# Seven products of summed sub-blocks in place of eight plain ones, in the second layer of a two-layer graph network on one Trainium2 core

## What is computed

```
x = layernorm(x + relu((adj / rowsum) @ x @ Wn.T + bn + x @ Ws.T + bs))
x = layernorm(x + relu(d * (adj @ (d * x)) @ W1 + b1))     d = rowsum ** -0.5
```

## Time and profile before

| what | value |
|---|---|
| median of 3 runs | 784.59 us (783.98 to 784.97) |
| the profiled execution, its own time | 784.35 us |
| its span, first to last instruction | 782.7 us |
| time outside the span | 1.65 us |
| TensorE matmul busy | 774.9 us (99%), 3672 instructions |
| VectorE busy | 597.9 us (76%), 951 instructions |
| ScalarE busy | 388.2 us (50%), 537 instructions |
| DMA | 160.93 MB, mean 206 GB/s |

### The profile page before, as it was taken

How to read it: one execution, slowest core, us unless ns; L and a number is a source line. 1 busy time by engine, 2 the same in 40 slices (tenths; PEclk the granted TensorE clock), 3 DMA queues, 4 the chain that set the end, 5 groups by cost and what they waited for, 6 DMA issues and landing times.

```text
span 782.7 us, 11147 instructions
## 1 busy us (share of the span) xinstructions
PE 774.9 (99%) x3672; PEld 647.7 (83%) x3672; DVE 597.9 (76%) x951; ACT 388.2 (50%) x537; POOL 2.5 (0%) x14
## 2 busy tenths in 40 slices
PE   9999999999999999999999999999999999999996
PEld 5888888888888888888888888888888888888886
DVE  6999999999899998998967565565646556564554
ACT  5644645646355464454644545454444545544452
POOL 0000000000000000000000000000000000000000
PEclk9999999999999999999999999999999999999999
DMA  7965574756646566475575656657574666657541
GB/s 297 340 242 190 197 260 162 246 183 198 231 151 244 171 200 237 149 244 186 187 246 176 231 171 215 213 189 242 171 248 150 211 213 194 236 180 242 165 165 52
DMA packets 54059, 160.93 MB, mean 206 GB/s; under 512 B 5008, under 2 KB 17936, under 8 KB 54032
## 3 DMA queue, kind: packets, MB, share of 16 engines
q1 hardware_dynamic: 45536, 151.41, 57.2%
q10 hardware_dynamic: 8352, 9.05, 3.4%
q0 software_dynamic: 144, 0.13, 0.1%
HBM read 152.17 MB, written 8.39 MB: 205 GB/s over the span
## 4 chain that ended last, share of the span: by engine, by line
PE 99%; DVE 0%; ACT 0%; issue 0%
PE ps_main L875 87%; PE ps_epi L795 6%; PE ps_epi L783 2%; PE ps_main L897 1%; PE ps_main L854 1%; PE ps_epi L786 1%; PE ps_main L842 1%; PE ps_epi L907 0%; DVE tt L531 0%; PE ps_epi L816 0%; DVE tt L552 0%; ACT ps_epi L418 0%; ACT tt L432 0%; DVE xs L773 0%; PE ps_epi L916 0%
## 5 line engine op out<-in xcount | busy, mean ns | idle before, releaser
L300 ACT ACTIVATE hi<-raw 128x1024 fp32r<-128x1024 f32 x254 | 268.9, 1059 | 277.2 <-PE ps_main L875 243.5
L474 DVE TENSOR_TENSOR lo<-raw,hi 128x1024 fp32r<-128x1024 f32 x254 | 310.3, 1222 | 98.0 <-ACT hi L300 97.8
L875 PE MATMUL ps_main<-hi,xs 128*128 128x512 f32 x1120 | 278.7, 391 | 0.0
L875 PEld LDWEIGHTS ps_main<-hi,xs 128*128 128x128 f32 x1120 | 208.0, 188 | 41.8 <-issue 0.5
L875 PE MATMUL ps_main<-hi,zs 128*128 128x512 f32 x880 | 217.7, 390 | 0.0
L875 PEld LDWEIGHTS ps_main<-hi,zs 128*128 128x128 f32 x880 | 164.0, 188 | 33.1
L875 PE MATMUL ps_main<-lo,xs 128*128 128x512 f32 x560 | 149.8, 390 | 0.0
L676 DVE TENSOR_TENSOR acc<-acc,raw 128x1024 f32<-128x1024 f32 x112 | 136.7, 1220 | 0.0
L875 PEld LDWEIGHTS ps_main<-lo,xs 128*128 128x128 f32 x560 | 105.2, 188 | 21.8
L875 PE MATMUL ps_main<-lo,zs 128*128 128x512 f32 x440 | 117.7, 390 | 0.0
L875 PEld LDWEIGHTS ps_main<-lo,zs 128*128 128x128 f32 x440 | 82.7, 188 | 17.1
(11 more groups left out here) (119 smaller groups left out, 373.7 us busy)
## 6 DMA issues: line engine op xcount, KB each, us to landing
raw<-adj_t SPq DMA_DIRECT2D x256, 512.0 KB, 3.3
res<-x_nat SPq DMA_DIRECT2D x11, 512.0 KB, 5.9
xt_sb<-xt SPq DMA_DIRECT2D x8, 512.0 KB, 5.6
x_scratch<-tt ACTq DMA_DIRECT2D x8, 512.0 KB, 4.2
res<-x_scratch SPq DMA_DIRECT2D x8, 512.0 KB, 6.1
out<-tt ACTq DMA_DIRECT2D x7, 512.0 KB, 6.7
tt<-x_nat SPq DMA_DIRECT2D x3, 512.0 KB, 4.2
acc<-x_nat ACTq DMA_DIRECT2D x1, 512.0 KB, 4.9
```

What stands on the lines that cost most here:

```text
L300: return act.activation(dst, src, ACT.Copy)
L474: return dve.tensor_tensor(dst, src, hi_part.bitcast(f32), ALU.subtract)
L875: last = pe.matmul(ps[:, f, :], stationary(layer, part, jt, f), mov[:, slot(u), cols], start=(jt == 0 and i == 0), stop=(jt == JT - 1 and ...
```

## The change

In blocks 1 to 6 of the second layer, the odd units 1, 3, ..., 13 (`SU`, seven units per block, 42 in all) are computed otherwise. A unit is a product of a 2 x 2 arrangement of feature sub-blocks (two tiles q by two feature halves f, each 128 x 128) with a 2 x 2 arrangement of `adj` sub-blocks (two tiles by two halves of 256 nodes, each 128 x 256). Before, it takes 8 products of sub-blocks, each in three passes. Now it takes seven products, some of them of sums of sub-blocks, each in three passes: 21 matmuls with 256 moving columns.

- **VectorE, once** (`t_sums`, `t_lo`; block 0): sums of feature sub-blocks for all seven units, in four groups, at units 5, 8, 11, 14, with ScalarE's `t_hi` between.
- **VectorE, per seven-unit** (`s_sums`, `s_lo`): four operations of 128 x 256 on `raw`, the third waiting for the first, the fourth for the third; placed behind `lo` of the unit before. Then the low part of the four sums, 128 x 1024. `lo` of the unit itself covers 768 columns instead of 1024.
- **ScalarE, per seven-unit** (`s_hi`): high part of the four sums, 128 x 1024, behind `hi` of the unit, which covers 768 columns.
- **PSUM.** Three of the products go straight to a half column of `ps_main`; four (`p1`, `p5`, `p6`, `p7`) are added up over the block in two tiles of `ps_epi` and belong to more than one result. In the next block ScalarE copies them out (`take_own`, 128 x 1024, unit 2), VectorE combines them in four operations of 128 x 256 (`join_own`, at (2,1), (2,2), (3,0)) and adds them to `ps_main` (`join_columns`, 128 x 1024, at (3,0)); then ScalarE's `st_hi` (`joined_columns`) and VectorE's `st_lo` (now at (3,1), behind `lo` of unit 3) follow.
- **TensorE** (`seven_products`): waits for `hi`, `lo` of the unit, high and low part of the sums, one after another. At the start of each block of the second layer but the first it waits for the squares of the block before.
- The epilogue's products go to two tiles of `ps_epi` and to `ps_main` of the finished block (`tile_sums`). The raw W1 weights for the last epilogue are loaded again in block 7, because `xt` is now in use.

The core of the diff:

```diff
+SU = tuple(range(1, 14, 2))
+NS = len(SU)
+SRING = 2
+T_UNITS = tuple(range(5, 16, 3))
...
+        def by_seven(layer, b):
+            return layer == 1 and not isinstance(b, int)
...
+            def joined_columns(e, parity):
+                act.wait_ge(c_ready, e + 1)
+                split_hi(st_hi[:, :, :], ps_main[parity][:, :, :]).then_inc(sth_ready, 1)
+
+            def take_own(e, parity):
+                act.wait_ge(own_zeroed, 1)
+                act.wait_ge(unit_done, (e + NB) * NU + (SU[-1] + 1))
+                act.activation(own_sbuf[:, :, :], ps_epi[:, parity * HT:(parity + 1) * HT, :], ACT.Copy).then_inc(own_ready, 1)
...
+            def s_hi(b, parity, u):
+                act.wait_ge(s_ready, s_index(b, parity, u) + 1)
+                split_hi(s_part(0, parity, u), acc[:, s_slot(parity, u), :]).then_inc(sh_ready, 1)
...
-                    split_hi(hi[:, slot(u), :], raw[:, slot(u), :]).then_inc(h_ready, 1)
+                    by_7 = by_seven(layer, b) and u in SU
+                    cols = slice(0, UW - HB if by_7 else UW)
+                    split_hi(hi[:, slot(u), cols], raw[:, slot(u), cols]).then_inc(h_ready, 1)
+                    if epi is not None and epi[0] == 1 and u == 2:
+                        take_own(epi[1], 1 - parity)
+                    if epi is not None and epi[0] == 1 and u == 3:
+                        joined_columns(epi[1], 1 - parity)
+                    if by_7:
+                        s_hi(b, parity, u)
+                    if layer == 1 and is_first(b) and u in T_UNITS:
+                        t_hi(T_UNITS.index(u))
...
+            def join_own(e, p):
+                p1, p6, p7, p5 = [own_sbuf[:, i // 2, i % 2 * HB:(i % 2 + 1) * HB] for i in range(4)]
+                if p == 0:
+                    dve.wait_ge(own_ready, e + 1)
+                    dve.tensor_tensor(p6, p1, p6, ALU.add).then_inc(u_chain, 1)
+                if p == 1:
+                    dve.wait_ge(u_chain, e * 4 + 1)
+                    dve.tensor_tensor(p7, p6, p7, ALU.add).then_inc(u_chain, 1)
+                if p == 2:
+                    dve.tensor_tensor(p6, p6, p5, ALU.add).then_inc(u_chain, 1)
+                    dve.wait_ge(u_chain, e * 4 + 2)
+                    dve.tensor_tensor(p5, p7, p5, ALU.add).then_inc(u_chain, 1)
+
+            def join_columns(n, e, parity):
+                dve.wait_ge(u_chain, e * 4 + 4)
+                dve.wait_ge(unit_done, (n + 1) * NU)
+                columns = ps_main[parity][:, :, :].rearrange("p f (r i) -> p f r i", i=HB)
+                own = own_sbuf[:, :, :].rearrange("p r (f i) -> p f r i", i=HB)
+                dve.tensor_tensor(columns, columns, own, ALU.add).then_inc(c_ready, 1)
...
+            def s_sums(b, parity, u):
+                k0 = b * (NU // RING) + NB * (NU // RING)
+                g = s_index(b, parity, u)
+                a12, a22, a11, a21 = [raw[:, slot(u), i * HB:(i + 1) * HB] for i in range(4)]
+                s1, s2, s3, s4 = [s_sum(parity, u, i) for i in range(4)]
+                dve.wait_ge(raw_full[slot(u)], (k0 + (u // RING + 1)) * 16)
+                dve.tensor_tensor(s3, a11, a21, ALU.subtract).then_inc(s_chain, 1)
+                dve.tensor_tensor(s1, a21, a22, ALU.add).then_inc(s_chain, 1)
+                dve.wait_ge(s_chain, g * 3 + 1)
+                dve.tensor_tensor(s2, a22, s3, ALU.subtract).then_inc(s_chain, 1)
+                dve.wait_ge(s_chain, g * 3 + 3)
+                dve.tensor_tensor(s4, a12, s2, ALU.subtract).then_inc(s_ready, 1)
+
+            def s_lo(b, parity, u):
+                dve.wait_ge(sh_ready, s_index(b, parity, u) + 1)
+                split_lo(s_part(1, parity, u), acc[:, s_slot(parity, u), :], s_part(0, parity, u)).then_inc(sl_ready, 1)
...
-                if (v, p) == (3, 0):
+                if (v, p) in ((2, 1), (2, 2), (3, 0)) and layer == 1:
+                    join_own(e, ((2, 1), (2, 2), (3, 0)).index((v, p)))
+                if (v, p) == (3, 0) and layer == 1:
+                    join_columns(n, e, parity)
+                if (v, p) == (3, 1 if layer else 0):
                     dve.wait_ge(sth_ready, n + 1)
                     split_lo(st_lo[:, :, :], ps_main[parity][:, :, :], st_hi[:, :, :]).then_inc(stl_ready, 1)
...
                     place(u, 1)
+                    if by_seven(layer, b):
+                        if u in SU:
+                            s_lo(b, parity, u)
+                        if u + 1 in SU:
+                            s_sums(b, parity, u + 1)
+                    if layer == 1 and is_first(b):
+                        if u in T_UNITS:
+                            t_lo(T_UNITS.index(u))
+                        if u + 1 in T_UNITS:
+                            t_sums(T_UNITS.index(u + 1))
+                        if u == NU - 1:
+                            dve.memset(ps_epi[:, 0:HT, :], 0.0).then_inc(own_zeroed, 1)
...
+            def seven_products(b, parity, u, g0):
...
+                pe.wait_ge(h_ready, g0 + (u + 1))
+                for i, part in enumerate((0, 1, 0)):
+                    if i == 2:
+                        pe.wait_ge(l_ready, g0 + (u + 1))
+                    mov = (hi, hi, lo)[i]
+                    for ps, st, at in plain:
+                        pe.matmul(ps, st(part), mov[:, slot(u), at * HB:(at + 1) * HB],
+                                  start=(ps is p1 and first and i == 0), stop=(ps is p1 and last_s and i == 2),
+                                  skip_group_check=(ps is p1))
+                pe.wait_ge(sh_ready, s + 1)
+                for i, part in enumerate((0, 1, 0)):
+                    if i == 2:
+                        pe.wait_ge(sl_ready, s + 1)
+                    mov = s_part((0, 0, 1)[i], parity, u)
+                    for n, (ps, st, at) in enumerate(summed):
+                        last = pe.matmul(ps, st(part), mov[:, at * HB:(at + 1) * HB],
+                                         start=(ps is p5 and first and i == 0), stop=(n > 0 and last_s and i == 2),
+                                         skip_group_check=(n > 0))
+                last.then_inc(unit_done, 1)
```

More of the change, by code:

```diff
@@ L177, in build, with tile_sums, own_sums, s_index @@
         w1_raw = xt[:, FH - 1, 0:F]
+        def by_seven(layer, b):
+            return layer == 1 and not isinstance(b, int)
+        def tile_sums(layer, e, parity, t):
+            if layer == 0 or isinstance(e, int) or t < HT:
+                own = 0 if layer == 0 or isinstance(e, int) else parity * HT
+                return ps_epi[:, own + t, :]
+            return ps_main[parity][:, t - HT, :]
+        def own_sums(parity, i):
+            return ps_epi[:, parity * HT + i // 2, i % 2 * HB:(i % 2 + 1) * HB]
+        own_sbuf = xt
+        def s_index(b, parity, u):
+            return b * NS + (SU.index(u) - NS)
+        def s_slot(parity, u):
+            return ((0 if parity == 1 else NS) + SU.index(u)) % SRING
+        def s_sum(parity, u, i):
+            return acc[:, s_slot(parity, u), i * HB:(i + 1) * HB]
+        def s_part(part, parity, u):
+            at = S_AT + s_slot(parity, u) * 4 + part * 2
+            return xs[:, at:at + 2].rearrange("p a c f -> p (a c f)")
+        def t_part(part, g, k):
+            return xs[:, T_AT + 2 * g + k // 2, part, k % 2 * P:(k % 2 + 1) * P]
+        def t_group(j):
+            return range(2 * j, min(2 * j + 2, NS))
         def moving_weight(layer, part, k):
@@ L531, in scale_product @@
                 ins = dve.scalar_tensor_tensor(
-                    out=tt[:, t, :], in0=ps_epi[:, t, at], scalar=(rdeg, d_cur)[layer][:, t:t + 1],
+                    out=tt[:, t, :], in0=(ps_epi[:, t, :] if sums is None else sums)[:, at], scalar=(rdeg, d_cur)[layer][:, t:t + 1],
                     in1=(bias0, bias1)[layer][:, :], op0=ALU.mult, op1=ALU.add)
@@ new lines, in t_lo @@
+            def t_lo(j):
+                gs = t_group(j)
+                rows = slice(T_AT + 2 * gs[0], T_AT + 2 * gs[-1] + 2)
+                dve.wait_ge(th_ready, j + 1)
+                split_lo(xs[:, rows, 1, :], acc[:, 1, 0:len(gs) * IB].rearrange("p (a f) -> p a f", f=F),
+                         xs[:, rows, 0, :]).then_inc(tl_ready, 1)
+            def s_sums(b, parity, u):
[10 more added lines that the diff above has]
+                dve.tensor_tensor(s4, a12, s2, ALU.subtract).then_inc(s_ready, 1)
@@ L845, in one_block @@
                     wait_x_split(pe, 0)
+                if layer == 1 and not is_first(b):
+                    pe.wait_ge(squares_ready, b * TB + (NB - 1) * TB)
                 for u in range(TAIL if ends else NU):
@@ L861, in one_block @@
                         pe.wait_ge(wl_ready, 3)
+                    if by_seven(layer, b) and u in SU:
+                        seven_products(b, parity, u, g0)
+                        epilogue(*epi, 1 - parity, u)
+                        continue
                     pe.wait_ge(h_ready, g0 + (u + 1))
```

79 lines of the change are left out of this document (64 added, 15 removed).

## The result

The changed kernel takes 786.02 us in the median of 20 runs (784.88 to 787.37) against 784.23 us of 20 runs of the kernel before: a ratio of 1.0023, 95% interval 1.0016 to 1.0030. It is slower, as forecast, but by 1.8 us and not by 4.9, and the difference is only just larger than the 0.2% that can be told from no change.

What follows compares the result with a forecast made beforehand. TensorE bound the kernel before; afterwards VectorE and ScalarE would: 43.7 work + 3.6 waits = 47.3 us per block. Block 1 at -0.1, blocks 2 to 6 at +1.0 each: +4.9 us, 784.59 becomes 789.5; range 780 to 797.

Steps and rivals of the forecast that it cites:

- TensorE's part: Second-layer blocks: a seven-unit takes 2.50 us instead of 2.72, a block 44.8 us; six blocks save 9.2 us.
- VectorE's part: VectorE's operations in one second-layer block, summed from distances between starts: 43.7 us, where it was about 26.
- the small steps: Seven or eight short VectorE operations per second-layer block, at 0.1 to 0.2 us each: 1.4 us.
- The waits, 3.6 us: VectorE's waits per block: sums and joins 1.0, s_lo 0.6, st_lo 0.3, lo of units 14 and 15 1.65 us.
- rival 3: Dearer hand-overs, 16 per round at 0.11 instead of 0.04 us, or join_columns at double: 796 us; chance 0.15.
- A round in which TensorE has no part: VectorE and ScalarE need 47.3 us per block; TensorE stands 2.3 to 2.5 us before the first wide product.
- rival 1: VectorE's added work stays hidden, its round below 44.8 us; TensorE's 9.2 us come in full: 775.4 us; chance 0.13.
- rival 2: Bound by VectorE with shorter waits: rounds 45 to 46.8 us, 776 to 786.2 us; chance 0.10 faster, 0.15 within 0.2%.
- "Hidden" work in block 0: VectorE's feature sums in block 0, about 13 us: 42 of some 49 us busy, costing nothing, otherwise once up to 2 us.
- The wait for `raw` at unit 3: raw lands in 3.3 us, needed over 6.5 us after its slot is free: costs nothing, up to a landing twice as long.
- A granted clock under 1.0 behind a stall: Sign of being wrong: TensorE idling with its granted clock under 1.0 behind the stall; no size given.
- Rival 4: Each VectorE operation starts only after the one before leaves the pipe: 0.08 us more for each of 56, 817 us; chance 0.02.

Runs made afterwards that it cites:

- experiment 1: Changed kernel plus one more 128x1024 VectorE operation per block of blocks 1 to 6, behind unit 9's low parts: 793.34 us, ratio 1.0119 against the kernel before.
- experiment 3: Changed kernel with the four join_own operations of each block left out, their sums missing from the result: 778.29 us, ratio 0.9924 against the kernel before.
- experiment 7's second form: Changed kernel with join_own on GpSimd and the copy of the own sums one unit earlier: 786.75 us, ratio 1.0031 against the kernel before.
- first form of experiment 6: Changed kernel with block 0's feature sums at units 5, 7, 9, 11 and the zeroing behind unit 12: 786.89 us, ratio 1.0031 against the kernel before.

## Why the prediction came out as it did

- **TensorE's part: right.** 2.50 us forecast, 2.51 measured; the block without waits is 45.02 and not 44.8, because a plain unit behind a seven-unit takes 0.03 us more, which no row of before could show.
- **VectorE's part, the step that failed: the sum of 43.7 us of VectorE work per block was too high by 0.9.** It took 42.8, so the round came to 46.4 and not 47.3. Two groups of terms were mis-sized. The accumulator read of each tile, four at 0.08, takes no distance of its own: in the earlier trace rows it starts at 506.46 and so does the next operation, and its 0.08 lies within the 0.35 already counted. And the small steps, put at 1.4 us, take 0.95: nine of them, at 0.06 to 0.10 from one start to the next where the next operation does not need the result, and at 0.19 to 0.21 where it does. The 256-column operations take 0.335, not 0.34. Together 0.3 + 0.45 + 0.15 = 0.9. The price of a small step could have been read before: the step at 221.48 in the earlier trace rows is followed, 0.06 later, by

```profile
221.54 1.22 DVE L676 TENSOR_TENSOR acc<-acc,raw 128x1024 f32<-128x1024 f32 x1
```

The small steps of the changed kernel, in units 11 and 12, where 578.91 to 579.20 are two of them and 577.37 to 577.45 one:

```profile
577.37 0.15 DVE L668 TENSOR_TENSOR newton<-newton,inv_root 128x4 f32<-128x4 f32 x1
577.45 0.42 DVE L742 TENSOR_TENSOR acc<-raw 128x256 f32<-128x256 f32 x1
...
578.91 0.15 DVE L671 SCALAR_TENSOR_TENSOR inv_root<-newton,inv_root 128x4 f32<-128x4 f32 x1
579.10 0.16 DVE L680 TENSOR_TENSOR nmr<-nmean,inv_root 128x4 f32<-128x4 f32 x1
579.20 0.96 DVE L565 TENSOR_TENSOR lo<-raw,hi 128x768 fp32r<-128x768 f32 x1
```
- **The waits, 3.6 us: right, each at its place.** Measured between the same starts: 0.80 and 0.79 at units 14 and 15, 0.34 and 0.27 at `s_lo` of 1 and 11, 0.06 at that of 13 (called covered), 0.32 at `st_lo`, 0.11 at each fourth sum, 0.2 at `join_columns`; together 3.6. Hand-overs were 0.03 or 0.04 but for one of 0.13 (`join_columns` behind the joins), so rival 3 did not come, and `join_columns` took 1.14 (547.83 to 548.97), as long as `st_lo`, which only reads PSUM: writing PSUM cost VectorE nothing extra here.
- **A round in which TensorE has no part: right.** Experiments 1 and 3 show both sides of the change-over at 45.0 us, so rival 1 is out. The result lies in rival 2's band, rounds of 45 to 46.8 us and 776 to 786.2, but not for its reason: the waits were as long as forecast, the work was shorter. The loss per block is the small difference of two large numbers, 46.43 against 46.31 where I had 47.3 against 46.3, so a 2% error in one sum made nearly all of the forecast 4.9 us: five rounds at +0.1 instead of +1.0. TensorE stands 1.0 to 1.2 us in an undisturbed block and not 2.3 to 2.5.
- **"Hidden" work in block 0: wrong by 0.75 us.** The count, 42 of 49 us, was right and the wrong question: the work lay on the way to `z_lo`. The wait for `raw` at unit 3, called free, came in two blocks of this execution, 0.46 us in block 1 and 0.41 in block 3, whose round is 0.7 us longer. Blocks 1 to 6 cost 1.6 us in this execution, 0.7 of it for `raw` in block 3, and block 0 another 0.75. Without these two terms, both of which the forecast had at nothing, about 0.3 us would be left, which cannot be told from no change: that the direction came out as forecast is luck in so far.
- **The clock.** A granted clock under 1.0 behind a stall was listed as a sign of being wrong. It came once in five stalls and, as shown above, did not lengthen the round.
- **Rival 4**, each operation starting only when the one before has left the pipe, is refuted further: the sums' starts are 0.335 apart with durations of 0.42.

## What to carry to other kernels

A saving on the bounding engine is worth only what the next engine's whole round leaves room for. That round is its work and its waits in series; it has to be compared to a few tenths of a per cent when the two are that close, and the sum must be made of distances between starts, in which a short instruction can cost less than its duration or nothing. To find out which engine paces, take one operation out and put one in, far from where the wait shows: if both move the time in full, the queue paces the kernel, and taking waits out of it by order alone (here 0.2 + 0.54 us a round and the head of the queue in block 0) turned a loss of 1.8 us into a gain of 5.5.

## What the runs showed of the hardware

- GpSimd's 128x256 adds on SBUF took 0.80 to 1.46 us in blocks 2 to 6 of experiment 7's second form (a trace gives GpSimd's times only roughly), and VectorE's two-operand operations beside them took up to 2.3 times as long (0.96 against 0.42).
- Behind a 1.83 us wait of TensorE the granted clock was 0.56 for 2.6 us, a mixture of its two levels, 1.2 and 2.4 GHz. Behind the 2.55 us wait in the first form of experiment 6 it was 0.53 for 3.5 us:

```profile
446.00:449.50 3.50, 3.50 (x11) 2.67 (x10) 3.47 (x7) 0.91 (x2) 0.00 (x0) 0.53 0.80 278
```

- Behind waits of 2.07 and 3.39 us in the profiled execution of experiment 1 it stayed 1.00. So the length of the wait alone does not decide it.
- Where the clock fell in the changed kernel, on an engine that had to wait for another anyway, it cost nothing: the next rounds of the pacing engine were 46.41 and 46.48 us as before. This is one case. The other three executions of experiment 1 had mean clocks of 0.992 to 0.994 against 0.998 and took 1.3 to 2.3 us longer than the profiled one; they have no trace, and whether the clock is the reason is open.
